# The expert stage's output deviations by a power on GpSimd, asked for between output transfers

## The reference

```python
x = hidden_states.reshape(-1, h)
logits = x @ w_router.T
_, top_idx = jax.lax.top_k(logits, TOP_K)            # TOP_K = 1
mask = jax.nn.one_hot(top_idx, E, dtype=logits.dtype).sum(axis=1)
scores = jax.nn.sigmoid(logits) * mask
masked_inputs = scores.T[:, :, None] * x[None, :, :]
gate_up = jnp.einsum('eth,ehf->etf', masked_inputs, gate_up_proj)
gate, up = jnp.split(gate_up, 2, axis=-1)
expert_out = jnp.einsum('etf,efh->eth', up * jax.nn.silu(gate), down_proj)
shared = jax.nn.silu(x @ w_gate.T) * (x @ w_up.T) @ w_down.T
out = shared + expert_out.sum(axis=0)
...
x = x + _layernorm(_L0_ffn_ref(_layernorm(x, axis=-1), ...), axis=-1)
```

## Time and profile before

| | us |
|---|---|
| median of 3 runs (312.31 to 313.1) | 312.32 |
| the profiled execution's own time | 313.13 |
| its span | 311.3 |
| busy in the span: PE / DVE / ACT / POOL | 269.1 / 268.7 / 191.5 / 187.5 |
| stage 3: first load issued, sum of row 0 | 216.11, 226.15 |
| first and last output transfer issued | 233.12, 308.77 |

### The profile page before, as it was taken

One profiled execution on the slowest core, in us unless ns is written; L12 is line 12 of the kernel. 1 busy time (PEld: TensorE's weight loads), 2 busy tenths in 40 slices (PEclk: granted clock), 3 DMA queues, 4 the chain that ended last, 5 costly groups with the idle time before them and its releaser, 6 DMA issues.

```text
span 311.3 us, 6412 instructions
## 1 busy us (share of the span) xinstructions
PE 269.1 (86%) x1569; PEld 192.2 (62%) x1569; DVE 268.7 (86%) x1073; ACT 191.5 (62%) x583; POOL 187.5 (60%) x204
## 2 busy tenths in 40 slices
PE   6777899999999999597599999989799999999700
PEld 3443556655555554344357666767799999999600
DVE  8899999999999999999879999660189999999940
ACT  2735466665666654336747776435798999999300
POOL 5556577777776777310005666754015788898776
PEclk9999999999999999799879999999799999999955
DMA  7999920000000000000002122223994101111100
GB/s 261 383 415 404 420 88 0 4 1 0 2 0 2 2 0 0 0 1 2 1 0 72 68 72 86 103 80 102 316 355 132 35 19 43 42 38 37 35 22 0
DMA packets 12491, 28.34 MB, mean 91 GB/s; under 512 B 2049, under 2 KB 8076, under 8 KB 11944
## 3 DMA queue, kind: packets, MB, share of 16 engines
q1 hardware_dynamic: 9408, 21.57, 18.9%
q0 software_dynamic: 3040, 6.37, 6.0%
q10 hardware_dynamic: 8, 0.00, 0.0%
HBM read 15.31 MB, written 13.60 MB: 93 GB/s over the span
## 4 chain that ended last, share of the span: by engine, by line
DVE 43%; PE 39%; issue 7%; POOL 4%; ACT 3%; DMA 2%; DVEq 0%; ACTq 0%; POOLq 0%; SPq 0%
PE banks L1262 13%; PE banks L1281 6%; DVE hT_e L1196 5%; DVE rows L1203 3%; DVE rows L1167 3%; PE banks L1319 2%; PE banks L1363 2%; DVE num L918 2%; POOL out L557 2%; PE banks L1298 2%; PE banks L1320 2%; DVE prod L894 2%; DVE stats L1218 2%; POOL sorted_rows L539 2%; PE banks L1442 2%
## 5 line engine op out<-in xcount | busy, mean ns | idle before, releaser
L514 POOL TENSOR_TENSOR kv<-qk,vv 128x1024 f32<-128x1024 f32 x32 | 62.5, 1953 | 2.5
L1262 PE MATMUL banks<-kv,upto 128*128 128x512 f32 x128 | 60.7, 597 | 1.0 <-POOL kv L514 1.0
L557 POOL DMA_INDIRECT out<-rows,token_i x47 | 47.0, 1000 | 10.6 <-issue 6.1
L1442 PE MATMUL banks<-xsT,w_now 128*128 128x128 f32 x376 | 52.5, 284 | 0.2
L539 POOL DMA_INDIRECT sorted_rows<-rows,slot_i x32 | 31.5, 984 | 27.3 <-ACT rows L664 12.3
L1442 PEld LDWEIGHTS banks<-xsT,w_now 128*128 128x128 f32 x376 | 47.1, 197 | 1.3 <-issue 1.0
L508 POOL TENSOR_TENSOR qk<-ex,rl 128x256 f32<-128x256 f32 x32 | 23.3, 729 | 36.8 <-ACT ex L612 36.8
L894 DVE TENSOR_TENSOR prod<-banks,qk 128x1024 f32<-128x1024 f32 x32 | 38.9, 1215 | 0.6 <-PE banks L1262 0.2
L918 DVE TENSOR_REDUCE num<-prod 128x128 f32<-128x1024 f32 x32 | 38.6, 1207 | 0.0
L1281 PE MATMUL banks<-w_qkvo,xnT 128*128 128x384 f32 x64 | 28.1, 521 | 6.1 <-DVE zq L880 3.9
L1262 PEld LDWEIGHTS banks<-kv,upto 128*128 128x128 f32 x128 | 22.3, 193 | 16.8 <-issue 15.6
(11 more groups left out here) (197 smaller groups left out, 649.2 us busy)
## 6 DMA issues: line engine op xcount, KB each, us to landing
sorted_rows<-rows SPq DMA_DIRECT2D x7, 780.0 KB, 13.7
rows<-sorted_rows SPq DMA_DIRECT2D x10, 520.0 KB, 6.6
w_exp<-in_gate_up SPq DMA_DIRECT2D x4, 1024.0 KB, 21.5
w_exp_out<-in_down SPq DMA_DIRECT2D x4, 512.0 KB, 21.7
x_then_down<-in_x SPq DMA_DIRECT2D x2, 768.0 KB, 6.4
out<-rows,token_i POOLq DMA_INDIRECT x47
sorted_rows<-rows SPq DMA_DIRECT2D x1, 650.0 KB, 19.6
x_then_down<-in_x SPq DMA_DIRECT2D x2, 256.0 KB, 3.3
```

Source lines behind the costliest of these rows:

```text
L514: nc.gpsimd.tensor_tensor(kv[:, u, :].rearrange("p (h m d) -> p h m d", h=NH, m=HD), k, v, ALU.mult).then_inc(s_kv, 1)
L557: nc.gpsimd.indirect_dma_start(out=out_rows, out_offset=bass.IndirectOffsetOnAxis(ap=token_i[:, j - 1:j], axis=0), in_=rows[:, j - 1, 0:D] ...
L1262: ins = nc.tensor.matmul(ps_s[u % 2][:, cols], upto[:], kv[:, u, cols], start=True, stop=True)
L1442: ins = nc.tensor.matmul(ps_gue[u % 2][:, c * P:(c + 1) * P], w_now[:, u % 2, c * P:(c + 1) * P], xsT[:, u % 2, :], start=True, stop=True)
```

## The change

DVE computes only the variances of a group (three steps). POOL raises them to the power -0.5, and DVE then scales each row and adds the residual in one instruction, for all 47 rows. POOL adds nothing any more. The groups are ten of 4 rows, then 3, 2 and 2. A group's power stands in POOL's program directly ahead of that group's first transfer, and so behind the last transfer of the group before. On DVE a group's first scaling stands one row after its variances. Beside that, SP no longer relays the loads' semaphores (ACT and DVE wait for the loads themselves), ACT copies the first two expert matrices ahead of the first tile, PE starts the first gate and up product before the second turn, and the one idle product becomes 20 + 44 products of 128 bf16 columns, 20 ahead of the wait for the scatters and 44 behind it.

```diff
-def scale_steps(nc, series, st, width, scratch, rs):
+def variance_steps(nc, series, st, width, scratch):
     yield series.done(tensor(t, mean_even, mean_even, ALU.mult))
     yield series.done(fused(out=ve, in0=sq_even, scalar=width * EPS, in1=sq_odd, op0=ALU.add, op1=ALU.add))
     series.wait()
-    yield series.done(fused(out=ve, in0=ve, scalar=1.0 / width, in1=t, op0=ALU.mult, op1=ALU.add))
-    series.wait()
-    yield series.done(scalar(y.bitcast(I32), ve.bitcast(I32), -0.5, RSQRT_MAGIC, ALU.mult, ALU.add))
...
-SCALE_STEPS = 11
+    yield fused(out=ve, in0=ve, scalar=1.0 / width, in1=t, op0=ALU.mult, op1=ALU.add)
+VARIANCE_STEPS = 3
...
-        ENDS = [2, 4, 6, 9, 12] + list(range(16, ST, 4)) + [ST]
+        ENDS = list(range(4, ST - 4, 4)) + [ST - 4, ST - 2, ST]
...
-            for j in range(ST + 1):
-                if j < ADDED_BY_POOL:
-                    x1 = flat(rows[:, j:j + 1, 0:D])
-                    pool.wait_ge(s_yn, j + 1)
-                    nc.gpsimd.tensor_tensor(x1, x1, flat(rows[:, j:j + 1, D:2 * D]), ALU.add).then_inc(s_fin, 1)
...
+            for j in range(ST):
+                for g, (j0, j1) in enumerate(GROUPS):
+                    if j0 == j:
+                        pool.wait_ge(s_variance3, g + 1)
+                        nc.gpsimd.tensor_tensor(rstd3[:, j0:j1], scratch3[:, 0, j0:j1], minus_half[:, 0:j1 - j0],
+                                                ALU.pow).then_inc(s_rstd3, 1)
+                pool.wait_ge(s_fin, j + 1)
+                if j in (0, TOKENS_FIRST):
+                    pool.wait_ge(s_token, 1 + (j > 0))
+                nc.gpsimd.indirect_dma_start(
...
-                dve.wait_ge(s_series3, SCALE_STEPS * (GROUP_OF[i] + 1))
-                if i < ADDED_BY_POOL:
-                    nc.vector.tensor_scalar(r, r, rstd3[:, i:i + 1], None, ALU.mult).then_inc(s_yn, 1)
-                else:
-                    nc.vector.scalar_tensor_tensor(out=x1, in0=r, scalar=rstd3[:, i:i + 1], in1=x1,
-                                                   op0=ALU.mult, op1=ALU.add).then_inc(s_fin_last, 1)
+                dve.wait_ge(s_rstd3, GROUP_OF[i] + 1)
+                nc.vector.scalar_tensor_tensor(out=x1, in0=r, scalar=rstd3[:, i:i + 1], in1=x1,
+                                               op0=ALU.mult, op1=ALU.add).then_inc(s_fin, 1)
...
-            nc.tensor.matmul(ps_idle[:], ident[:], w_g_u[:, 0:4 * P], start=True, stop=True)
+            def stay_warm(count):
+                for _ in range(count):
+                    nc.tensor.matmul(ps_idle[:, 0:P], ones_bf[:], ones_bf[:], start=True, stop=True)
+            stay_warm(20)
             pe.wait_ge(s_scattered, 16 * NT)
+            stay_warm(44)
```

More of the change, by code:

```diff
@@ new lines, in turned_row, with silu_row @@
+            def turned_row(j):
+                if j < ST:
+                    act.wait_ge(s_xs_t, j + 1)
+                    at_least(act, s_gue, j - 1)
+                    nc.scalar.copy(xsT[:, j % 2, :], ps_xs[:, 0:D]).then_inc(s_xsT, 1)
+            def silu_row(j):
+                if j < ST:
+                    act.wait_ge(s_gue, j + 1)
+                    at_least(act, s_he, j - 1)
+                    nc.scalar.activation(silu_e[:, j % 2, :], ps_gue[j % 2][:, 0:F], ACT.Silu).then_inc(s_silue, 1)
@@ new lines, in _ @@
+            weights(0, expert_of(0))
+            weights(1, expert_of(1))
+            normed_row(0)
+            turned_row(0)
+            normed_row(1)
+            for j in range(ST):
+                e = expert_of(j + 2)
+                if j == 0:
+                    turned_row(j + 1)
+                    silu_row(j)
+                    normed_row(j + 2)
+                elif j == 1:
+                    silu_row(j)
+                    turned_row(j + 1)
+                    normed_row(j + 2)
+                else:
+                    normed_row(j + 2)
+                    turned_row(j + 1)
+                    silu_row(j)
+                weights(j + 2, e)
@@ L1176, in tokens, with scale_up_to @@
                                         ).then_inc(s_token, 1)
+            def scale_up_to(i):
+                nonlocal scaled
+                while scaled < i:
+                    scale_row(scaled)
+                    scaled += 1
             begun, scaled = 0, 0
             chain = iter(())
-            left = 0
-            def chain_steps(count):
-                nonlocal left
-                for _ in range(count):
-                    if left:
-                        next(chain)
-                        left -= 1
@@ L1189, in _ @@
-            for j in range(-2, ST + 1):
+            for j in range(-2, ST):
                 u = j % 4
-                many, most = begun in (1, 2, 3), begun == 1
                 if live(j + 2, ST):
@@ L1454, in _ @@
             pe.wait_ge(s_experts, 1)
             pe.wait_ge(s_centred_e, E // CENTRED_AT_ONCE)
-            run_quads(pe, step3, -1, 1, 9, QUADS)
+            turn(0)
+            gate_up(0)
+            gate_up(1)
+            turn(2)
+            for j in range(ST):
+                e = pe.value_load(tile_expert[0:1, j:j + 1], min_val=0, max_val=E - 1)
+                turn(j + 3)
+                gate_up(j + 2)
+                down_row(j, e)
 _INS = ["x", "w_att", "b_qkv", "bo", "w_ffn", "gate_up", "down"]
```

200 lines of the change are left out of this document (78 added, 122 removed).

## The result

| | before | changed |
|---|---|---|
| median of the runs, us | 312.36 | 320.06 (319.87 to 320.34, 4 runs) |
| the profiled execution's own time, its span | 313.13, 311.3 | 319.87, 318.1 |
| sum of row 0; first and last output transfer issued | 226.15; 233.12, 308.77 | 225.23; 233.04, 315.61 |

The account below looks back on a forecast made before the run. The prediction took POOL's queue of transfers to bound the end. From 232.8, spacings of 44.3, group changes of 32.6 and a last transfer of 0.98, less 0.3, end at 310.4, 0.65 later than before: 313.0, range 311.1 to 315.2.

Parts of the forecast that it names:

- the break: On POOL, from the start of a group's last transfer to the next group's first: 2.72 us against a plain 1.304.
- DVE's end to the transfer that waited: Between groups, from the end of DVE's scaling to the start of POOL's waiting output transfer: 0.28 us.
- the narrow ones: Powers of 3, 2 and 2 columns in the last groups, taken to save 0.3 us together.
- The 34 spacings within groups: On POOL, output transfers following one of their own group, at 1.304 us each: 44.3 us.
- The first transfer: POOL's first output transfer, forecast at 232.8 where it was 233.12 before.
- The start: First rows of the stage: idle products to 219.5, clock kept up, sum of row 0 at 225.7, 0.45 us earlier.
- its two ends: Sum of row 0: 0.7 us earlier if all is kept, 0.2 us later if the clock falls again.
- The second: POOL between groups: slower transfer after a wait or slower power, 0.15 us more per group change, 314.8; chance 0.14.
- the third: POOL between groups: quicker transfer start and perhaps cheap narrow powers, 2.0 us less, 311.0; chance 0.14.
- The fourth: POOL's power costs only what a product costs, 9.8 us less, 303.2; chance 0.04.
- The fifth: At the start, PE's idle products run at the lower clock, 3.4 us later, 316.4; chance 0.05.
- the sixth: DVE reaches each group's scaling 0.3 us after the power, 3.6 us more, 316.6; chance 0.05.

## Why the prediction was wrong

**The step that failed** is one term of the break: "DVE's end to the transfer that waited: 191.95 to 192.23, 0.28 us". It is 0.80. The mechanism, a series of power, scaling and transfer, was right; this term of it was mis-sized. The transfer of the earlier trace rows carries its wait itself; the output transfer's wait stands on the register instruction ahead of it, and 0.79 us pass from the release to the transfer's start. The code has the difference, since only the output transfer has a bounds check, and the earlier trace rows hid it: behind an add or a transfer that instruction is released early. With the wait moved onto the transfer the 0.28 of the prediction came back (0.29). Twelve breaks by 0.52 us are 6.2 us.

**The sum, term by term.** Nine breaks of 3.24 us and three of 3.08, 2.93 and 2.93 make 38.1, against 32.3: 5.8 more. The powers are 1.06 for 1.03, the narrow ones save 0.8 for the 0.3 taken. The 34 spacings within groups are 315.61 - 233.04 - 38.1 = 44.5, against 44.3. The first transfer is at 233.04, against 232.8; it too starts 0.8 us after its scaling, and a start of the stage that is 0.5 us earlier than forecast hides most of that. The last one ends at 316.6, against 310.4.

**Own time and median.** From own time to own time the change costs 319.87 - 313.13 = 6.7 us, against 0.65. From median to median it costs 7.7: the profiled execution of before lay 0.8 above its median, that of after 0.2 below. The prediction moved the difference over unchanged, which is the last microsecond of the miss.

**What held.** Power, scaling and transfer stand in series and nothing hides them. DVE is idle ahead of the scalings and never late itself, though by 2.2 us a group and not the 0.7 given. POOL's loop is longer than PE's, and the chain alternates between POOL and DVE to the last row. The start came in the way worked out: idle products to 219.2, the clock at 1.00 over 222 to 223, and sum of row 0 at 225.23, earlier than the 225.7 and a little outside its two ends. One reading of the lines was off without harm: 298.99 is the start of the first of DVE's last three scalings. They end at 299.87, 8.9 us and not almost ten before POOL's last transfer starts.

**The rivals.** The second ("the break is dearer") is what happened, but with 0.15 us per break where 0.52 came; its mechanism, a slower transfer or a slower power, did not (1.04 and 1.06 us). None of the seven names the start behind a register instruction; the 0.14 for a dearer break had the sign right by another cause. Of the third only the cheap narrow powers came. The fourth is out: the power takes 1.06 us, the product in its place 0.20. The price in the Trainium skill ("GPSIMD Engine Reference", 3.1) does not hold for the power of this kernel, which took 0.15 us for each column. The fifth and the sixth did not occur.

## What to carry to other kernels

When an engine issues a transfer with a wait, look at which instruction carries it: a wait on a helper instruction ahead of the transfer adds its whole start to the path, here 0.5 us each time the wait is late. A latency read from one transfer holds for another only if both are built alike and both really waited. And an operation taken off a busy engine is no gain when it lands in series on the engine whose queue ends the kernel. Issued one transfer earlier, this one left the scaling under a transfer; what that is worth in time was not shown.

## What the runs showed of the hardware

- A power on GpSimd takes 0.76, 0.90 and 1.06 us for 2, 3 and 4 columns, by which 0.15 us a column stand on top of 0.45. A product of the same operands takes 0.20 to 0.24.
- An indirect transfer released late starts 0.79 to 0.87 us after the release when the wait is on the register instruction ahead of it, whether POOL had computed a power or a product or had stood idle for 3.8 us, and 0.29 when it carries the wait.
- The same kernel took 320 us on one chip and 336 to 341 on others, while the kernel before moved only from 312.4 to 316 to 317. With an addition of 0.48 us between output transfers many of the late starts went away in both kernels in which it was tried (DVE's waits for the down product from 18.5 to 1.2 us in one, POOL's waits ahead of the powers from ten to one in the other).
